# A sequence-model block with mixture-of-experts layers: from all eight experts for every token to the two chosen ones, sorted by expert through DRAM

## The chip, the cores and the metric

The kernel runs on one core of one Trainium2 chip. The metric is the device time of one execution in microseconds (us); a profiled execution is shown beside it, with the time from its first to its last instruction (the span).

The engines are named as in the profile: PE is the matmul engine, PEld its weight load, DVE the vector engine, ACT the engine of activations, POOL the engine that also builds descriptors for its own DMAs, SP the one that only issues DMAs and waits.

## The reference, cut to what matters

Sixteen sequences of 256 tokens, 128 features wide, go through an FFN, a mixer and a second FFN, with residual sums. Each FFN is a mixture of eight experts of which each token uses two; it is this part that the change rewrites.

```python
def ffn(x, gate_w, w1s, w2s):                 # x normalised; E = 8, D = 128, H = 512
    logits = xf @ gate_w
    probs = softmax(logits)
    vals, idx = top_k(probs, 2)
    vals = vals / sum(vals)                   # weights of the two chosen experts
    combine = zeros((N, E)).at[arange(N)[:, None], idx].add(vals)
    out = zeros_like(xf)
    for e in range(E):
        h = silu(xf @ w1s[e])
        out += combine[:, e:e + 1] * (h @ w2s[e])
    return out
```

The mixer is two Mamba blocks (a projection, a short convolution, a scan over time with 16 states for each of 256 channels, a projection back), the second with a small memory read on top:

```python
def step(h, ins):                             # over the 256 tokens of a sequence
    h = h * exp(d_t[:, :, None] * A) + (d_t * u_t)[:, :, None] * B_t[:, None, :]
    return h, einsum('bds,bs->bd', h, C_t)
```

## The kernel before, in words

Tokens are worked in eight groups of two sequences (512 tokens, four tiles of 128). A group has four slots, one for each sequence in each of the two Mamba blocks. The engines run programs written out by hand: `ORDER` gives for each engine, and each of the four slots, the order of its steps, and `run` plays the four slots for each group. Between engines there are only semaphores, and each engine keeps its order, so a step that waits holds all that stand behind it on its engine.

The scan of a slot is cut in eight steps j, each with two states for two halves of the channels (1024 elements in each of 128 partitions). For each j, ACT makes the decays (step `d`, line 621), PE spreads two rows over the partitions (steps `t`, line 403, into a ring of three banks `b_r`), and DVE does three large operations: the input product (`b`, line 900), the scan itself (`s`, line 910) and the output product (`g`, line 922). The output products of j = 1 to 7 are added by DMA: POOL issues one accumulating DMA for each (steps `a`, `pair_sum`, line 1098, 512 KB from `G` onto `acc`). Each of these waits until the one before it has landed, and `G` has three buffers (`NG = 3`), so the g step of j waits for the landing of an earlier one. The step `gate` (line 930) takes the finished sum of the slot before, so it waits for the seventh DMA.

Around the scan stand the small steps: on DVE `low`, `delta`, `xsum`, `un`, `lx`, `ln`, `unx`, `mask`, `xb`; on POOL the reciprocal roots `froot`, `rms`, `lnx`, `rmsx` (an add, a drain of the engine, and a power, lines 1066 and 1068) and the residual `rs`.

Sixteen FFNs (two for each group) are laid into the slots: the first stands alone ahead of the mixer (`start`), the last alone behind it (`finish`), and the fourteen others each take two slots. Of one FFN, before:

- DVE normalises (`fstats`, `fnorm`), takes the low part of the split tokens (`flow`), reads the logits (`flog`), takes the two largest (`ftop`) and makes an 8-wide row of weights (`fweights`).
- PE works in 64 pieces (steps `p`): for each expert four up pieces, each of three matmuls of 512 columns (the tokens and weights are split in a high and a low part), and four down pieces of 16 matmuls of 128 columns.
- ACT applies silu to 32 tiles of 512 columns (line 564).
- DVE adds each expert's result with the token's weight (`ffn_sum`, line 836): four operations for each of eight experts, from PSUM.

The weights of all experts stay in SBUF. PE, ACT and DVE run groups 1 to 5 as a loop (`Fori`); SP and POOL have them written out.

Of the kernel before, what the change touches and what calls it, by code (L numbers as in the profile page):

```python
# [5 lines left out]
P = 128  # L6
# [3 lines left out]
SEQ = 2  # L10
# [14 lines left out]
        ("outside", PAD)]  # L25
# [9 lines left out]
PAIR = 4 * HC  # L35
PIECES = E // 2 * PAIR

# [17 lines left out]
    ),  # L55
    "scalar": (
# [4 lines left out]
    ),  # L61
    "vector": (
# [35 lines left out]
def moe_mamba_kernel(nc, x, pack, early, sel, w1, w2, out):  # L98
# [4 lines left out]
    with ctx:  # L103
# [5 lines left out]
        raw = sb("raw", [P, E * HID])  # L109
        w1h = sb("w1h", [P, E, HID], fp32r)  # L110
        w1l = sb("w1l", [P, E, HID], fp32r)
        w2s = sb("w2s", [P, E, HC, D])
        selr = sb("selr", [P, 2 * DS, P], fp32r)
        ghl = sb("ghl", [P, 2, E], fp32r)
# [10 lines left out]
        def par(name):  # L125
# [13 lines left out]
        xh = sb("xh", [P, TOK], fp32r)  # L139
        xl = sb("xl", [P, TOK], fp32r)  # L140
# [65 lines left out]
        s_pack, s_w1, s_w2, s_sel, s_early, s_gate = (  # L206
            sem("s_pack"), sem("s_w1"), sem("s_w2"), sem("s_sel"), sem("s_early"), sem("s_gate"))
        s_raw_read, s_lg, s_Aexp, s_set_dve, s_set_act, s_exponent = (
            sem("s_raw_read"), sem("s_lg"), sem("s_Aexp"), sem("s_set_dve"), sem("s_set_act"),
            sem("s_exponent"))  # L210
        s_xin, s_store = sem("s_xin"), sem("s_store")

        f_stats, f_rstd, f_xn, f_xnT, f_split, f_logits, f_lread, f_gap, f_th, f_xh = (
            sem("f_stats"), sem("f_rstd"), sem("f_xn"), sem("f_xnT"), sem("f_split"),
            sem("f_logits"), sem("f_lread"), sem("f_gap"), sem("f_th"), sem("f_xh"))
        f_hmm, f_hact, f_ymm, f_yacc = sem("f_hmm"), sem("f_hact"), sem("f_ymm"), sem("f_yacc")
# [15 lines left out]

        def piece(k):

            pair, i = divmod(k, PAIR)
            down, i = divmod(i, 2 * HC)
            return bool(down), 2 * pair + i // HC, i % HC
# [25 lines left out]
        def _(sp):  # L263
# [16 lines left out]

            for g in range(GROUPS):
                if g + 1 < GROUPS:
                    sp.wait_ge(f_yacc, first(g) * E + 1)
                    sp.dma_start(xin[:, :, :], xt[g + 1]).then_inc(s_xin, 16)
                if g >= 2:
                    store(g - 2)
            store(GROUPS - 2)
            store(GROUPS - 1)
            sp.wait_ge(s_store, 16 * GROUPS)


        @block.tensor
        def _(pe):
# [34 lines left out]
            def ffn_down(n, e, j):  # L328
# [6 lines left out]
                if j == TILES - 1:  # L335
                    last.then_inc(f_ymm, 1)
# [869 lines left out]
```

## Time and profile before

| | us |
|---|---|
| median of three runs (1804.24 to 1805.67) | 1805.59 |
| the profiled execution's own time | 1800.28 |
| its span, first to last instruction | 1798.5 |
| DVE busy | 1585.3 (88%) |
| PE busy | 1472.0 (82%) |
| ACT busy | 1170.0 (65%) |
| POOL busy | 307.3 (17%) |

The profile has a page with shares, forty slices of the span and the costliest groups of instructions; behind it the trace can be asked for the instructions of a stretch, for who waited for whom, and for the DMAs. "Busy" counts instructions that compute; issuing a DMA counts on POOL alone. An engine that is idle and is not the bound costs nothing, so the shares tell where to look, and the waits tell what sets the end.

### The profile page before, as it was taken

To read this page: it belongs to the slowest core of one execution; us is meant where nothing else is said; L and a number is where in the kernel's file an instruction comes from. 1 tells how busy PE (TensorE), PEld (TensorE's weight loads), DVE (VectorE), ACT (ScalarE), POOL (GpSimd) and SP (SyncE) were. 2 spreads that over 40 slices of the span, in tenths; PEclk is the share of its full clock that TensorE was granted. 3 is DMA by queue.
4 is the path that set the end of the run, shared out by engine and by line. 5 is a ranking of instruction groups with operands and counts; after the bars stand their busy time and mean duration, and the time that the engine had idled before them with its cause. 6 is when DMAs were issued, how large, how long until landed. Compare 5 with 4: busy or idle time off the path is not lost. (4 is left out here: it accounts for less than half of the span.)

```text
span 1798.5 us, 26359 instructions
## 1 busy us (share of the span) xinstructions
PE 1472.0 (82%) x8672; PEld 1260.7 (70%) x8672; DVE 1585.3 (88%) x2421; ACT 1170.0 (65%) x2227; POOL 307.3 (17%) x366
## 2 busy tenths in 40 slices
PE   5878666888989888988889788888889898568768
PEld 4767545777777778777778678776778677447657
DVE  5249999999999999999999999999999999999821
ACT  3267555866866777866876677856876677558422
POOL 0001121122112221122112121122112121111100
PEclk9988866998999899998999899998999899569979
DMA  5004444433443334433443334433344334443400
GB/s 198 1 12 82 77 82 82 88 71 59 83 84 71 71 71 90 89 71 60 80 87 67 74 72 90 87 68 62 74 80 78 67 75 89 82 82 73 94 5 7
DMA packets 43947, 131.93 MB, mean 73 GB/s; under 512 B 3984, under 2 KB 12176, under 8 KB 43664
## 3 DMA queue, kind: packets, MB, share of 16 engines
q0 software_dynamic: 32256, 117.45, 34.4%
q1 hardware_dynamic: 11536, 12.56, 2.2%
q8 instruction: 79, 1.29, 0.3%
q14 instruction: 76, 0.62, 0.1%
HBM read 10.46 MB, written 2.10 MB: 7 GB/s over the span
## 5 line engine op out<-in xcount | busy, mean ns | idle before, releaser
L910 DVE TENSOR_TENSOR_SCAN hs<-dA,dbu 128x1024 f32<-128x1024 f32 x256 | 584.3, 2288 | 5.2 <-issue 3.6
L564 ACT ACTIVATE raw<-b_h 128x512 f32<-128x512 f32 x512 | 304.2, 599 | 268.4 <-PE b_h L326 255.7
L621 ACT ACTIVATE dA<-delta,A 128x255 f32<-128x255 f32 x1024 | 421.7, 495 | 12.1 <-DVE hs L910 9.9
L1098 POOL DMA_DIRECT2D acc<-G x224 | 195.9, 875 | 1028.8 <-DVE G L922 583.5
L403 PE MATMUL b_r<-bcr,selr 128*128 128x256 f32 x1024 | 243.9, 334 | 124.7 <-DVE G L922 65.8
L324 PE MATMUL b_h<-xh,w1h 128*128 128x512 f32 x512 | 247.9, 484 | 82.1 <-DVE ob L836 29.3
L900 DVE TENSOR_TENSOR dbu<-du,b_r 128x1024 f32<-128x1024 f32 x256 | 306.2, 1206 | 6.6 <-PE b_r L403 4.3
L403 PEld LDWEIGHTS b_r<-bcr,selr 128*128 128x128 f32 x1024 | 177.3, 207 | 166.9 <-DVE G L922 75.3
L922 DVE TENSOR_TENSOR G<-hs,b_r 128x1024 f32<-128x1024 f32 x224 | 272.0, 1214 | 7.1 <-issue 5.0
L333 PE MATMUL b_out<-w2s,raw 128*128 128x128 f32 x2048 | 252.2, 275 | 0.0
L333 PE MATMUL b_h<-w2s,raw 128*128 128x128 f32 x2048 | 250.2, 275 | 0.0
L333 PEld LDWEIGHTS b_out<-w2s,raw 128*128 128x128 f32 x2048 | 244.8, 192 | 4.1
L333 PEld LDWEIGHTS b_h<-w2s,raw 128*128 128x128 f32 x2048 | 241.1, 192 | 1.1
L326 PE MATMUL b_h<-xh,w1l 128*128 128x512 f32 x512 | 219.8, 429 | 0.0
L325 PE MATMUL b_h<-xl,w1h 128*128 128x512 f32 x512 | 219.6, 429 | 0.0
L324 PEld LDWEIGHTS b_h<-xh,w1h 128*128 128x128 f32 x512 | 107.0, 209 | 159.8 <-ACT raw L564 71.5
L361 PE MATMUL b_w<-uT,inx 128*128 128x256 f32 x512 | 153.4, 440 | 9.4 <-ACT ez L610 4.5
L326 PEld LDWEIGHTS b_h<-xh,w1l 128*128 128x128 f32 x512 | 107.1, 209 | 26.7
L361 PEld LDWEIGHTS b_w<-uT,inx 128*128 128x128 f32 x512 | 103.9, 220 | 24.5 <-ACT uT L574 6.1
L325 PEld LDWEIGHTS b_h<-xl,w1h 128*128 128x128 f32 x512 | 109.0, 213 | 9.0
L621 ACT ACT_TABLE_LOAD x86 | 110.3, 1283 | 1.5
L564 ACT ACT_TABLE_LOAD x44 | 56.5, 1283 | 24.3 <-PE b_h L326 23.7
(144 smaller groups left out, 1551.6 us busy)
## 6 DMA issues: line engine op xcount, KB each, us to landing
acc<-G POOLq DMA_DIRECT2D x224, 512.0 KB, 4.5
xin<-x_dram SPq DMA_DIRECT2D x8, 256.0 KB, 2.8
raw<-w_dram SPq DMA_DIRECT2D x1, 2048.0 KB, 10.9
out_dram<-ob SPq DMA_DIRECT2D x8, 256.0 KB, 2.9
prm<-pack_dram SPq DMA_DIRECT2D x1, 1124.5 KB, 5.2
hs<-sel_dram SPq DMA_DIRECT2D x2, 512.0 KB, 12.3
G<-sel_dram SPq DMA_DIRECT2D x2, 512.0 KB, 7.5
dA<-early_dram SPq DMA_DIRECT2D x1, 512.0 KB, 11.4
```

The costliest lines, as they stand in the source:

```text
L324: mm(h, w1h[:, e, w], xh[:, :], start=True, stop=False)
L325: mm(h, w1h[:, e, w], xl[:, :], start=False, stop=False)
L326: mm(h, w1l[:, e, w], xh[:, :], start=False, stop=True).then_inc(f_hmm, 1)
L333: last = mm(EOUT[e % 2][:, j * D:(j + 1) * D], hT[e % 2][:, c, j * P:(j + 1) * P], w2s[:, e, c, :], start=c == 0, stop=c == HC - 1)
L361: last = mm(o, inx[:, m, r, ch], uT[:, b, PAD - r:PAD - r + T], start=r == 0, stop=r == PAD)
L403: last = mm(R[ring(i, t)][:, d * T:(d + 1) * T], selr[:, kind * DS + DP * j + d, :], bcr[b][:, :], start=True, stop=True)
L564: do(hT[e % 2][:, c, :], H[i % 2][:, :], ACT.Silu).then_inc(f_hact, 1)
L621: last = do(dA[j % 4][:, d, k, 1:], delta[b][:, k, 1:], ACT.Exp, scale=A[:, k, s:s + 1])
L900: V.tensor_tensor(dbu[j % 2][:, :, :, :], du[i % 2][:, :, :].unsqueeze(1).broadcast_to([P, DP, HALVES, T]), spread_rows(i, (0, j)), ALU.mu ...
L910: V.tensor_tensor_scan(flat(hs[j % 2]), flat(dA[j % 4]), flat(dbu[j % 2]), 0.0, ALU.mult, ALU.add)\
L922: V.tensor_tensor(to[:, :, :, :], hs[j % 2][:, :, :, :], spread_rows(i, (1, j)), ALU.mult)\
L1098: Q.dma_start(acc[b][:, :, :, :].rearrange("p d h t -> p (d h t)"), G[j % NG][:, :, :, :].rearrange("p d h t -> p (d h t)"), accum_op=ALU. ...
```

## The change

Each FFN computes each token for its two experts only. Its parts:

- The first matmul runs in full fp32, no longer in split parts; the copies `w1h`, `w1l`, `xh`, `xl` and the operations that make them go.
- After the two largest logits, DVE makes a 0/1 mask, PE counts by matmul how many tokens come before each one at each expert, and DVE works out a place for each (token, expert) pair in a list of `NT` = 15 tiles of 128 rows in which each expert starts on a tile of its own (`ffn_place`), and the expert of each tile (`eid`).
- POOL scatters the 4 x 128 normalised tokens to their two places in DRAM with eight indirect DMAs (`ffn_scatter`, 64 KB each), after which SP loads the sorted list back in five chunks of three tiles (`chunk_in`).
- For each of the 15 tiles SP reads the expert's number from SBUF into a register and loads that expert's first weight, 256 KB, from DRAM into a ring of four (`expert_in`); PE turns the tiles (15 transposes), does 4 up matmuls of 128 columns, reads the expert's number into a register, and does 4 down matmuls; ACT does 15 silus and 10 copies from PSUM.
- SP writes the results to DRAM in five chunks (`chunk_out`), and POOL gathers them back with eight indirect DMAs (`ffn_gather`). DVE adds them with 8 operations from SBUF in place of 32 from PSUM.
- Routing (norm, logits, places, scatter) now stands in the slot before the two that hold the matmul pieces, and the sums stand at the end of the second of these. All four `ORDER` lists are new. POOL has 7 accumulating DMAs in every slot as before, and 16 indirect ones more in slots 1 and 3.
- POOL copies the residual once for each FFN (`ffn_keep`), and the two sorted lists are cleared once at the start. The loop on PE, ACT and DVE is written out.

```diff
-        "rms a1 rs froot a2 a3 a4 a5 a6 a7",
-        "rms a1 rs lnx a2 a3 rmsx a4 a5 a6 a7",
-        "a1 a2 froot a3 a4 a5 a6 a7",
+        "froot a1 a2 sc0 sc1 sc2 sc3 sc4 sc5 fkeep rms a3 sc6 sc7 a4 ga0 ga1 ga2 ga3 ga4 a5 ga5 ga6 ga7 rs a6 a7",
+        "rms a1 a2 a3 rs a4 lnx a5 rmsx a6 a7",
+        "froot sc0 sc1 sc2 a1 a2 sc3 sc4 a3 sc5 a4 sc6 ga0 ga1 ga2 sc7 ga3 a5 ga4 ga5 ga6 ga7 a6 fkeep a7",
...
+        "b0 b1 s0 s1 g0 gate b2 g1 s2 b3 b4 s3 g2 low s4 g3 delta b5 mask g4 s5 b6 g5 b7 xb s6 s7 g6 g7",
+        "b0 b1 s0 fstats s1 g0 b2 fnorm s2 flog g1 ftop b3 fplace g2 gate s3 xsum b4 b5 g3 un s4 g4 b6 s5 s6 g5 "
+        "b7 g6 fweights s7 low g7 fsum delta",
+        "b0 b1 s0 b2 g0 gate s1 xsum g1 b3 un s2 lx g2 s3 b4 g3 s4 b5 g4 s5 b6 g5 s6 ln low g6 b7 unx delta s7 g7",
+        "fstats b0 b1 fnorm s0 flog b2 ftop g0 fplace s1 g1 s2 b3 g2 gate s3 b4 g3 s4 b5 g4 s5 low b6 g5 b7 s6 "
+        "delta mask g6 s7 fweights g7 fsum xb",
...
             def ffn_up(n, e, c):
...
-                mm(h, w1h[:, e, w], xh[:, :], start=True, stop=False)
-                mm(h, w1h[:, e, w], xl[:, :], start=False, stop=False)
-                mm(h, w1l[:, e, w], xh[:, :], start=False, stop=True).then_inc(f_hmm, 1)
+            def ffn_up(n, i):
+                r, k, t = RING_OF["U", i], n * NT + i, i % CH * P
+                pe.wait_ge(s_w[k % NW], 16 * (k // NW + 1))
+                wait(pe, f_hact, n * ITEMS + max(r - 1, RING_OF["T", i // CH] + 1))
                 for c in range(HC):
+                    w = slice(c * P, (c + 1) * P)
+                    last = mm(H[r % 2][:, w], wst[k % NW][:, w], xsT[i // CH % 2][:, t:t + P], start=True, stop=True)
+                last.then_inc(f_hmm, 1)
+
+            def ffn_down(n, i):
+                pe.wait_ge(f_hact, n * ITEMS + RING_OF["U", i] + 1)
...
+                e = pe.value_load(eid[n % 2][0:1, i:i + 1], min_val=0, max_val=E - 1)
+                for c in range(HC):
+                    last = mm(Y[:, i % CH * D:(i % CH + 1) * D], hT[i % NH][:, c, :], w2s[:, e, c, :],
+                              start=c == 0, stop=c == HC - 1)
+                last.then_inc(f_ymm, 1)
...
+            def ffn_sum(f):
+
+                n, src, dst, g, is_first = f
+                dve.wait_ge(s_gat, 16 * 2 * TILES * (n + 1))
...
                 for k in range(2):
...
+                    for j in range(TILES):
+                        last = V.scalar_tensor_tensor(
+                            out=dst[:, j, :], in0=yk[:, k, j, :], scalar=c01[n % 2][:, k, j:j + 1], in1=dst[:, j, :],
+                            op0=ALU.mult, op1=ALU.add)
...
+            def ffn_scatter(n, x):
+                k, j = divmod(x, TILES)
+                if x == 0:
+                    pool.wait_ge(f_pos, n + 1)
+                    pool.wait_ge(s_zero, 32)
+                Q.indirect_dma_start(xs_d[n % 2], bass.IndirectOffsetOnAxis(ap=posi[n % 2][:, x:x + 1], axis=0),
+                                     xn[:, j, :], None).then_inc(s_scat, 16)
+
+            def ffn_gather(n, x):
+                k, j = divmod(x, TILES)
+                if x == 0:
+                    wait(pool, f_yacc, n)
+                    for c in range(CHUNKS):
+                        pool.wait_ge(s_ys[c], 16 * (n + 1))
+                Q.indirect_dma_start(yk[:, k, j, :], None, ys_d[n % 2],
+                                     bass.IndirectOffsetOnAxis(ap=posi[n % 2][:, x:x + 1], axis=0)).then_inc(s_gat, 16)
```

## Rows read from the trace of the kernel before

**Rows 1.** Windows of the span: busy us of each engine, clock, DMA share, GB/s.
```profile
0.00:114.00 114.00, 74.32 (x414) 60.47 (x415) 37.82 (x136) 35.63 (x60) 6.34 (x17) 0.92 0.23 79
114.00:1705.00 1591.00, 1328.52 (x7861) 1143.92 (x7861) 1529.45 (x2212) 1112.07 (x2130) 298.87 (x346) 0.90 0.40 77
```

**Rows 2.** Timeline of SP, stores of successive groups: start, us, engine, line, operation.
```profile
505.89 0.39 SPq L279 DMA_DIRECT2D out_dram<-ob  x1
...
1114.85 0.38 SPq L279 DMA_DIRECT2D out_dram<-ob  x1
```

**Rows 3.** DVE: groups by line of the middle stretch, then its timeline in one slot.
```profile
L910 DVE TENSOR_TENSOR_SCAN hs<-dA,dbu 128x1024 f32<-128x1024 f32 x256 | 584.3, 2288 | 5.2 <-issue 3.6 <-ACT dA L621 0.2
L922 DVE TENSOR_TENSOR G<-hs,b_r 128x1024 f32<-128x1024 f32 x224 | 272.0, 1214 | 7.1 <-issue 5.0 <-DVE hs L910 1.0 <-DMA acc<-G 0.4
...
914.84 0.68 DVE L788 TENSOR_TENSOR xl<-b_out,xh 128x512 fp32r<-128x512 f32 x1
...
928.67 0.19 DVE L824 TENSOR_TENSOR comb<-hit 128x32 f32<-128x32 f32 x1
...
937.50 1.12 DVE L836 SCALAR_TENSOR_TENSOR xa<-b_out,comb,xin 128x128 f32<-128x128 f32 x4
938.54 1.21 DVE L922 TENSOR_TENSOR G<-hs,b_r 128x1024 f32<-128x1024 f32 x1
```

**Rows 4.** A slot that holds no FFN: its window, POOL's timeline, and DVE's gate behind it.
```profile
268.50:308.40 39.90, 24.00 (x93) 19.55 (x94) 37.85 (x37) 22.80 (x50) 7.59 (x9) 0.66 0.49 93
...
277.34 0.86 POOL L1098 DMA_DIRECT2D acc<-G  x1 [4.18 <-DMA acc<-G]
...
282.23 1.04 POOL L1068 TENSOR_TENSOR rstd<-rstd,powh 128x4 f32<-128x4 f32 x1 [3.58 <-DMA acc<-G]
283.23 0.89 POOL L1098 DMA_DIRECT2D acc<-G  x1
288.36 0.86 POOL L1098 DMA_DIRECT2D acc<-G  x1 [4.24 <-DMA acc<-G]
...
308.36 0.69 DVE L930 TENSOR_TENSOR yg<-acc 128x512 f32<-128x512 f32 x1 [0.64 <-DMA acc<-G]
```

**Rows 5.** DMA queue and issues; last row: accumulates beside a store, 904 to 916 us.
```profile
q0 software_dynamic: 32256, 117.45, 34.4%
...
acc<-G POOLq DMA_DIRECT2D x224, 512.0 KB, 4.5
xin<-x_dram SPq DMA_DIRECT2D x8, 256.0 KB, 2.8
...
DMA to landing us min/median/max: 4.9/5.2/5.4
```

**Rows 6.** POOL's adds at line 1066, two of one shape: ns min/median/max.
```profile
L1066 POOL TENSOR_TENSOR rstdm<-mvm,epst x7: 2238/2242/2247, 226.8 to 1437.2; 128x4 f32<-128x4 f32 x7
L1066 POOL TENSOR_TENSOR rstdr<-vr,epst x7: 201/201/203, 244.1 to 1456.6; 128x4 f32<-128x4 f32 x7
```

**Rows 7.** ACT by line: silu and the table loads ahead of it.
```profile
L564 ACT ACTIVATE raw<-b_h 128x512 f32<-128x512 f32 x512 | 304.2, 599 | 268.4 <-PE b_h L326 255.7
...
L564 ACT ACT_TABLE_LOAD x44 | 56.5, 1283 | 24.3 <-PE b_h L326 23.7
```

**Rows 8.** The FFN alone at the start, DVE: normalised, last sum, first scan input.
```profile
9.61 1.12 DVE L780 TENSOR_SCALAR xn<-xin,mv,rstd 128x128 f32<-128x128 f32 x4 [1.19 <-POOL rstd L1068]
...
84.32 1.13 DVE L836 SCALAR_TENSOR_TENSOR xa<-b_h,comb,xa 128x128 f32<-128x128 f32 x4 [2.45 <-PE b_h L333]
...
114.16 1.22 DVE L900 TENSOR_TENSOR dbu<-du,b_r 128x1024 f32<-128x1024 f32 x1
```

**Rows 9.** The FFN alone at the end: DVE normalised and last sum, PE 32 down matmuls.
```profile
1728.76 1.12 DVE L780 TENSOR_SCALAR xn<-xb,mv,rstd 128x128 f32<-128x128 f32 x4 [2.64 <-POOL rstd L1068]
...
1793.78 1.13 DVE L836 SCALAR_TENSOR_TENSOR ob<-b_h,comb,ob 128x128 f32<-128x128 f32 x4 [2.45 <-PE b_h L333]
...
1743.41 3.73 PE L333 MATMUL b_out<-w2s,raw 128*128 128x128 f32 x32
```

More of the change, by code:

```diff
@@ L24 @@
         ("out_b_row", D), ("ident", P), ("dist", T), ("causal", T), ("iota", E), ("tap_b", DI), ("ones_row", P),
-        ("outside", PAD)]
+        ("outside", PAD), ("before", P), ("steps", TILES), ("tiles", 15), ("ones_e", E)]
 DP = 2
@@ L277, in store, with chunk_out, load_x @@
+            def chunk_out(n, c):
+                wait(sp, s_gat, 16 * 2 * TILES * (n - 1))
+                sp.wait_ge(f_ys, n * CHUNKS + c + 1)
+                sp.dma_start(rows(ys_d[n % 2], c), ys[:, c * CH:(c + 1) * CH, :]).then_inc(s_ys[c], 16)
+            def load_x(g):
+                sp.wait_ge(f_keep, first(g - 1) + 1)
+                sp.wait_ge(f_xn, first(g - 1) + 1)
+                sp.dma_start(xin[:, :, :], xt[g]).then_inc(s_xin, 16)
             def store(g):
-                sp.wait_ge(f_yacc, (second(g) + 1) * E)
+                sp.wait_ge(f_yacc, second(g) + 1)
@@ L279, in store @@
                 sp.dma_start(ot[g], ob[:, :, :]).then_inc(s_store, 16)
[L281 to L287, printed above, removed]
+            firsts = {first(g): g for g in range(GROUPS)}
+            seconds = {second(g): g for g in range(GROUPS)}
+            for n in range(2 * GROUPS):
+                for i in range(NW):
+                    expert_in(n, i)
+                if n in seconds and n - 1 in seconds:
+                    store(seconds[n - 1])
+                for c in range(CHUNKS):
+                    chunk_in(n, c)
+                if n in firsts and firsts[n] + 1 < GROUPS:
+                    load_x(firsts[n] + 1)
+                if n in firsts and n - 1 in seconds:
+                    store(seconds[n - 1])
+                for i in range(NW, NT):
+                    expert_in(n, i)
+                    if i >= CH + 5 and i % CH == 2:
+                        chunk_out(n, (i - 5) // CH - 1)
+                for c in range((NT - 1 - 5) // CH, CHUNKS):
+                    chunk_out(n, c)
@@ L342, in turn @@
                 wait(pe, q_sp, 4 * g + i)
+                if i == 0 and 0 < g < GROUPS - 1:
+                    pe.wait_ge(f_tile, first(g + 1) + 1)
+                elif i == 2 and g > 0:
+                    pe.wait_ge(f_tile, second(g - 1) + 1)
                 for j in tiles:
@@ L525, in _ @@
             run(0, first(1), None, first(2), False)
-            with pe.Fori(1, GROUPS - 2) as g:
+            for g in range(1, GROUPS - 2):
                 run(g, g * 2, g * 2 + 1, g * 2 + 2, False)
@@ L691, in _ @@
             run(0, first(1), None, first(2), False)
-            with act.Fori(1, GROUPS - 2) as g:
+            for g in range(1, GROUPS - 2):
                 run(g, g * 2, g * 2 + 1, g * 2 + 2, False)
@@ L1049, in _ @@
             run(0, first(1), None, first(2), False)
-            with dve.Fori(1, GROUPS - 2) as g:
+            for g in range(1, GROUPS - 2):
                 run(g, g * 2, g * 2 + 1, g * 2 + 2, False)
@@ L1107, in residual, with slot @@
                 Q.tensor_tensor(rs[:, tiles, :], xam[:, tiles, :], x1[:, tiles, :], ALU.add).then_inc(g_rs, 1)
-            def slot(g, i, tail, head, n, nx, nxt):
+            def slot(g, i, tail, head, f, fx, nxt):
                 for name, num in steps("gpsimd", i):
@@ L1139, in run @@
                     head = (g, i + 1) if i < 3 else None if is_last else (g + 1, 0)
-                    slot(g, i, tail, head, (n1, n2)[i // 2], (n2, n3)[i // 2], None if is_last else g + 1)
+                    slot(g, i, tail, head, (f1, f2)[i // 2], (f2, f3)[i // 2], None if is_last else g + 1)
             start()
@@ L1177 @@
         "gate": a("ffn_gate_w"),
+        "before": (np.arange(P)[None, :] > s).astype(f), "ones_e": np.ones((P, E), f),
+        "steps": np.broadcast_to(P * np.arange(TILES, dtype=f), (P, TILES)),
+        "tiles": np.broadcast_to(np.arange(NT, dtype=f), (P, NT)),
         "xp": rows(np.concatenate([bc, xp[:DR].T], 1)), "out_w": rows(a("attn_out_proj_w").T),
```

444 lines of the change are left out of this document (272 added, 172 removed), and 26 rows, old and new, of the table ORDER.

## The prediction

> **What bounds the kernel now.** I read the windows of the span first. The kernel has a head until the first scan input at 114 us, a middle to 1705 us, and a tail. In the middle DVE is busy 1529 of 1591 us, PE 1329, ACT 1112, POOL 299 [rows 1]: DVE is the bound there, at 96%. The reader is to see that PE, which loses most work by the change, is not. Then SP's timeline, for the period: three groups pass between the stores at 505.89 and 1114.85 us, so a group takes 203.0 us, a slot 50.7 [rows 2]. Then DVE by line and in order: the scan is 2.29 us, the two products 1.21 each, and neighbours overlap by some 0.09 us (four sums take 1.12 us and the next operation starts 1.04 after them) [rows 3]. So one j is about 4.45 us, eight are 35.6: 70% of a slot is scan that no part of the change touches.
>
> The third view matters most: the one slot of the middle where PE has no FFN and DVE hardly any. It runs at a granted clock of 0.66 with PE busy 24 of 39.9 us, and DVE is still busy 37.9; but the accumulating DMAs go back to back, 5.13 us from 283.23 to 288.36, and the gate behind them waits 0.64 us for the last [rows 4]. So just below DVE lies a second bound: the chain of seven DMAs, each of which waits for the landing of the last. At 5.05 us each it needs 35 us, and with what stands between the gate and a1 a slot can't be shorter than about 39. One more thing is seen there: POOL's power at 282.23 waited 3.58 us for the DMA issued ahead of it, and that pair of issues is 5.89 apart. A root on POOL (add, drain, power) finishes only when DMAs issued before it have landed.
>
> **DVE's own work, per FFN.** Removed: 32 sums, 8 x 1.04 = 8.3 us, of which 8 come back as sums from SBUF, taken at the same 0.26 each = 2.1. Removed: the low part, 0.6 with overlap; one read of logits and the two products with the weights, about 0.75 (four small operations of 0.19 with drains) [rows 3]. Added: some ten small operations in the place step with a drain between most, at 0.19 plus 0.08 each, about 2.4. Net 8.3 + 0.6 + 0.75 - 2.1 - 2.4 = 5.2 us saved, 10.4 for a group. PE loses most of its FFN: 57 us of matmuls become about 15, since 32 matmuls of the down kind take 3.73 us and there are now 120 of them and 15 transposes [rows 9]. As DVE is the bound, that alone gives nothing.
>
> From this, and the new order, DVE's slots without any wait are: slot 0, 40.5 us; slot 1, 50.4; slot 2, 44.8; slot 3, 49.2. Sum 185. The FFN's DVE work stands in slots 1 and 3 alone, so 0 and 2 come close to the floor of 39.
>
> **What the chain of DMAs becomes.** Three new loads fall on it.
>
> (a) Traffic. For each FFN there are 15 weight loads of 256 KB, 1.97 MB of chunks in and out, and 1.05 MB scattered and gathered: 6.9 MB, 27 transfers of 256 KB, 13.3 for a slot. A store of 256 KB beside the accumulates raised their landing from 4.5 us to 5.4 at most [rows 5]: up to 0.9 us for one. An accumulate holds the DMA engines for 2.76 us (34.4% of 1798.5 over 224) [rows 5], seven are 19.3 of 50 us, so 39% of 13.3 x 0.9 = 12 us meets them: 4.6 us for a slot, 0.65 for each. Bounds: 0 (all transfers fall in gaps) and 1.15 (in proportion to the time in flight). I take 0.65: landing 5.15, period 5.7.
>
> (b) Sixteen indirect issues in slots 1 and 3. The nearest row is the direct issue on POOL, 0.86 us [rows 4]. An indirect one must also fetch 128 numbers, so it isn't cheaper. The upper bound is from POOL's adds: the same 128x4 add takes 201 ns in one place and 2242 in another, where DVE runs a scan [rows 6]. If a fetch were held so, on half of the issues, one would be 1.9. I take 1.1, near the direct row. The Trainium skill (SBUF — State Buffer, Who interferes with whom) says that a DVE instruction with two SBUF inputs contends with a GpSimd one that reads SBUF, and that the second to issue blocks; the two rows agree. By that rule, if it holds for index fetches, 1.9 is the price and the time is that of the second rival. Landing of an indirect DMA: none is shown; the nearest is 2.8 us for 256 KB [rows 5], which I take.
>
> (c) The roots. They now stand behind the last accumulate of the slot before, or behind scatters.
>
> Now the four slots, times from each slot's start. Slot 0: gate ends about 9.9, g1 at 12; a7 is issued at 12 + 6 x 5.7 = 46.2, which is 5.7 in slot 1, and lands at 10.9. froot ends a microsecond later, 11.9; DVE wants fnorm at 10.0: wait 1.9. Slot 1: about one microsecond each of round trip to PE before flog and before fplace; places at 23.7, a2 at 24.8, six scatters to 32.3, their landing 35.1, the root of `rms` to 36.1 (un waits 1.5), a3 there, a4 at 41.8, five gathers to 48.2, a5, three gathers to 52.4, landed 55.2. DVE wants fsum at 52.2: wait 3.0. Slot 1 = 50.4 + 2 + 1.9 + 1.5 + 3.0 = 58.8. Slot 2: g1 at 14.2; lnx and rmsx add 2.5 to the chain; a7 at 50.9, 6.1 into slot 3, lands 11.3; froot 12.3. DVE wants fnorm at 3.4, since fstats opens the slot: wait 8.9. This is the largest new wait; behind it on DVE stand the whole scan of slot 3 and, on PE, the turn, the logits and the counts. Slot 3: places at 24.1, three scatters to 27.4, a1 27.4, a2 33.1, a3 38.8, a4 44.5, six indirect ones to 52, a5, four gathers to 57.3, landed 60.1; DVE wants fsum at 57.5: wait 2.6. Slot 3 = 49.2 + 2 + 8.9 + 2.6 = 62.7. Sum 40.5 + 58.8 + 44.8 + 62.7 = 206.8 against 203.0: +3.8 for a group. What is idle as dispatch gaps today (some 5 us of a group) I count as covered by the new waits. The middle has 32 slots less those with less FFN, about seven such groups: **+27 us**.
>
> **Head and tail.** At the tail, from xn to the last sum, now 1729.9 to 1794.9 = 65.0 us [rows 9]. After: turn, gate, top, counts, places about 11; eight scatters 8.8 and landing 2.8; chunk in 3.2; 15 tiles; chunk out 3.2; eight gathers 8.8 and landing 2.8; sum 2.1. A tile: up 0.45 (4 x 0.117, less overlap), silu 0.6 and two semaphore hops 0.3 [rows 7], the register load, down 0.45. No row shows a register load on PE; bounds 0 and 1.5 (then SP, with one load and one issue of 0.4 for each tile, would bind as well), taken 0.9: 2.7 for a tile, 40.5, with turns and copies 42.5. Sum 85.4: **+20**. The Trainium skill (DMA: Bandwidth & Descriptors, Latency and other measured facts) has about 600 ns as the floor of a tensor load; with 0.6 the two lone FFNs are 9 us cheaper in all. At the head the same 85.4 from xn at 10.7 ends at 96.1, before 85.5 [rows 8]: +10.6; the second FFN's routing now lies between the norm and the first turn of the mixer, 5.5 less the 2.3 of norm work moved ahead: **+14** in all. Clearing the lists (2 x 0.98 MB) stands ahead of the other loads on SP's queue but lands before the places are known.
>
> Work that is hidden: the ten copies and the silus on ACT (15 x 0.6 + 10 x 0.4 in place of 32 x 0.6); table loads rise by my count from 25 to 36 for a group, 11 x 1.28 = 14 us more on an engine that is busy 70% [rows 7, 1]. In slot 1 ACT would then be busy 45 of 59 us: covered, and without that cover up to 7 us for a slot. The lower clock: covered, as the slot at 0.66 shows [rows 4].
>
> **Sum.** 27 + 20 + 14 = 61. On the profiled execution's 1800.3 that is 1861; the median stands 5 above it, so 1866 us, +3.4%.
>
> **Rivals.**
> - *The chain keeps its pace (faster).* Issue 0.86, no traffic met: the same walk gives waits of 2 and 0.6 in slot 1, 4.3 and 2 in slot 3, slots 40.5 + 53 + 44.8 + 55.5 = 193.8, seven times -9.2 = -64, head and tail +24: 1766. For it: DMA engines are busy 40% only [rows 1]. Against: the chain had no slack in the slot without FFN [rows 4], and slots 0 and 2 become such slots. It decides at about 0.3 us of traffic for each accumulate with 1.0 for an issue; there the group is near 199 and the time 1806, no change.
> - *Indirect issues are held (much slower).* At 1.9 each, 0.8 more on 16 issues puts about 11 us into each of slots 1 and 3: +150 in the middle, +26 at the ends: 2040. At 1.5, 1950.
> - *PE's register loads hold the spread rows.* 15 loads of 1.5 us with the waits ahead of them put 11 us into each slot of PE, in order with the `t` steps. PE has 20 us to spare in a slot, but where five pieces stand ahead of t0 a bank can be late by 3 us: +80 over the middle, 1945 if all else is as forecast.
> - *It doesn't do what it says:* if the PE work did not fall, nothing of the middle would change beyond the above, as DVE binds; this would show in PE's busy time only.
>
> **How the numbers follow.** Forecast (chain late by some, 1820 to 1930) 0.50; chain keeps its pace 0.32 (with 0.27 below 1802); held issues 0.10; PE 0.08. A run can tell 0.2%, 3.6 us. Within it falls little from either side: 0.05. Faster 0.30, slower 0.65. The range reaches from the first rival, 1755 with cheap register loads, to 1960 (held issues at 1.5); beyond it remain the issues above 1.5 us and some of the first rival's best.
>
> **What would show it.** Right: DVE's wait at fnorm, on POOL's root, and at the sum, on gathers, are the largest of the middle; accumulates land in over 5 us; DVE busy about 70 us less in the middle; PE busy under 900. Wrong: indirect issues under 0.9 or over 1.5 on POOL; DVE waiting for `b_r`; head and tail moved by less than 15 or more than 60 together.

## The result and the profile after

The changed kernel takes 2034.28 us (median of 2033.62 to 2043.89); the kernel before, on the same chip, 1805.63. The ratio is 1.127, with an interval from 1.124 to 1.131: slower, by 229 us where +61 was forecast, and outside the range. The profiled execution has a span of 2032.8 us.

| us | before | after |
|---|---|---|
| DVE busy | 1585.3 (88%) | 1497.6 (74%) |
| PE busy | 1472.0 (82%) | 1292.5 (64%) |
| ACT busy | 1170.0 (65%) | 1176.6 (58%) |
| POOL busy | 307.3 (17%) | 640.0 (31%) |
| start to the first scan input | 114.2 | 130.5 |
| from there to the last norm (`xn`) | 1614.6 | 1810.4 |
| from there to the end of the last sum | 66.2 | 89.2 |

The three last rows (each from where the one above ends) say where the 234 us between the two spans lie: 16 at the head, 196 in the middle, 23 at the tail. Head and tail were forecast at 14 and 20; the middle at 27. The windows of after answer to [rows 1], columns as there:

```profile
0.00:130.50 130.50, 57.93 (x356) 52.41 (x356) 29.62 (x147) 31.17 (x55) 33.94 (x44) 0.84 0.47 143
130.50:1912.00 1781.50, 1185.79 (x6705) 1052.07 (x6704) 1453.40 (x1933) 1128.58 (x2106) 586.37 (x574) 0.79 0.55 121
1912.00:2032.80 120.80, 48.78 (x317) 44.51 (x317) 14.55 (x66) 16.88 (x31) 19.65 (x22) 0.67 0.27 72
```

DVE's busy time in the middle fell by 76 us (third number with its count: 1453.40 against 1529.45; 73 between the same two steps, first scan input and last norm, 1460.51 against 1533.87). It is now busy 82% of the middle, and no other engine is busier: none is the bound by its work alone. So the next view is that of the waits. First the length of a group, from DVE's gates two groups apart (timeline):

```profile
638.05 0.68 DVE L1040 TENSOR_TENSOR yg<-acc 128x512 f32<-128x512 f32 x1
...
1104.20 0.68 DVE L1040 TENSOR_TENSOR yg<-acc 128x512 f32<-128x512 f32 x1
```

That is 233.1 us a group against 203.0 in [rows 2] and 206.8 forecast. The window of just these two groups:

```profile
638.05:1104.20 466.15, 317.49 (x1847) 283.86 (x1846) 371.37 (x530) 297.86 (x551) 164.65 (x158) 0.81 0.56 126
```

What DVE waited for in it (line, releaser: us in total, times, longest):

```profile
DVE ob L945 <- DMA yk<-results,posi: 21.9, 2, 11.3
DVE xn L874 <- POOL rstd L1173: 12.9, 4, 3.9
DVE xa L945 <- DMA yk<-results,posi: 12.2, 2, 6.3
DVE un L976 <- POOL rstdr L1173: 8.4, 4, 4.9
DVE lg L880 <- PE b_w L386: 6.3, 4, 1.6
DVE un L976 <- issue: 6.2, 2, 3.2
DVE more L905 <- PE b_w L397: 5.8, 4, 2.1
DVE ln L959 <- POOL rstdm L1173: 4.4, 2, 2.7
DVE acc L1032 <- PE b_r L500: 3.7, 2, 2.2
```

DVE is busy 371.37 / 2 = 185.7 us of a group (the forecast's slots without waits sum to 185). The waits are 86.2 / 2 = 43.1, forecast 21.9; 4.3 more lie between its instructions. The largest are the sums on the gathered rows (`ob`, `xa`: 17.0 us a group). The norms on POOL's roots follow: `un`, 7.3, and `xn`, 6.5. (The `un` waits marked `issue` belong there: they are 22.3 us in the whole trace, and 3.4 in `e4_own_sem` below, whose roots have no drain.) `b_r` is small. POOL stands behind sums and norms. Its groups by line (busy us, mean ns, idle before with releasers), and then its timeline in a slot 3:

```profile
L1230 POOL DMA_DIRECT2D acc<-G x224 | 204.1, 911 | 822.8 <-DMA acc<-G 427.0 <-DVE G L1032 395.4 <-issue 0.3
L1194 POOL DMA_INDIRECT sorted<-xn,posi x128 | 178.7, 1396 | 140.4 <-DVE posi L928 104.0 <-issue 36.4
L1203 POOL DMA_INDIRECT yk<-results,posi x128 | 162.1, 1267 | 117.8 <-DMA results<-ys 80.0 <-issue 36.0 <-DMA acc<-G 1.8
```

```profile
731.17 0.20 POOL L1171 TENSOR_TENSOR rstd<-mv,epst 128x4 f32<-128x4 f32 x1
734.87 1.03 POOL L1173 TENSOR_TENSOR rstd<-rstd,powh 128x4 f32<-128x4 f32 x1 [3.50 <-issue]
748.93 2.87 POOL L1194 DMA_INDIRECT sorted<-xn,posi  x1 [13.03 <-DVE posi L928]
752.11 1.01 POOL L1194 DMA_INDIRECT sorted<-xn,posi  x1 [0.30 <-issue]
...
762.10 1.05 POOL L1194 DMA_INDIRECT sorted<-xn,posi  x1 [0.30 <-issue]
763.45 3.04 POOL L1194 DMA_INDIRECT sorted<-xn,posi  x1 [0.30 <-issue]
766.49 0.99 POOL L1230 DMA_DIRECT2D acc<-G  x1
...
790.15 0.95 POOL L1203 DMA_INDIRECT yk<-results,posi  x1 [0.30 <-issue]
```

And DVE in the same stretch:

```profile
748.60 2.29 DVE L1020 TENSOR_TENSOR_SCAN hs<-dA,dbu 128x1024 f32<-128x1024 f32 x1
...
763.37 2.28 DVE L1020 TENSOR_TENSOR_SCAN hs<-dA,dbu 128x1024 f32<-128x1024 f32 x1
...
794.15 2.35 DVE L945 SCALAR_TENSOR_TENSOR ob<-yk,c,ob 128x128 f32<-128x128 f32 x8 [11.28 <-DMA yk<-results,posi]
```

Two things are to be seen. The scatter at 763.45 starts just after the scan at 763.37 and takes 3.04 us, to 0.84 us past the scan's end; its neighbour at 762.10, with no scan, takes 1.05. Over the whole trace, 61 of the 256 indirect issues start in a scan and have a mean of 2.41 us; the 195 others have 0.99, and only one of these is over 1.2 (1.99, at 27.77, beside `scalar_tensor_tensor` operations of DVE). To each comes a gap of 0.30 us. So an issue costs 1.33 + 0.30 = 1.63 us on average, and the last gather of this slot is issued at 790.15, when DVE has been waiting for it since 782.87. The second thing: the root's power at 734.87 idles 3.50 us behind an add that ended at 731.37. The last sign of landing of the accumulate issued just ahead of it, at 730.16, comes 0.2 us before the power starts. In the kernel before, 14 such powers start 0.17 or 0.38 us after the landing of the accumulate issued ahead of them.

### The profile page after: what moved, and what is told of

Read it like the earlier page. It is cut to its first block and busy times, and to the rows that moved or that the text cites. A ratio compares the mean times of both kernels' runs of the same rounds, so it can differ in the third digit from the quotient of the medians.

```text
span 2032.8 us, 26140 instructions
## 1 busy us (share of the span) xinstructions
PE 1292.5 (64%) x7376; PEld 1149.0 (57%) x7376; DVE 1497.6 (74%) x2145; ACT 1176.6 (58%) x2191; POOL 640.0 (31%) x639
## 5 line engine op out<-in xcount | busy, mean ns | idle before, releaser
L423 PE MATMUL b_out<-w2s,hT 128*128 x1920 | 296.4, 303 | 72.0 <-issue 45.9
L414 PE MATMUL b_h<-xsT,wst 128*128 128x128 f32 x1920 | 303.6, 310 | 57.6 <-ACT xsT L667 40.8
L414 PEld LDWEIGHTS b_h<-xsT,wst 128*128 128x128 f32 x1920 | 280.2, 224 | 65.9 <-issue 65.6
L423 PEld LDWEIGHTS b_out<-w2s,hT 128*128 128x128 f32 x1920 | 266.8, 215 | 88.2 <-issue 87.8
L1010 DVE TENSOR_TENSOR dbu<-du,b_r 128x1024 f32<-128x1024 f32 x256 | 305.8, 1209 | 14.6 <-PE b_r L500 10.7
L670 ACT ACTIVATE hT<-b_h 128x512 f32<-128x512 f32 x240 | 140.7, 598 | 172.9 <-PE b_h L414 164.6
L458 PE MATMUL b_w<-uT,inx 128*128 128x256 f32 x512 | 178.9, 497 | 69.8 <-DVE xb L1070 61.7
L1194 POOL DMA_INDIRECT sorted<-xn,posi x128 | 178.7, 1396 | 140.4 <-DVE posi L928 104.0
L1203 POOL DMA_INDIRECT yk<-results,posi x128 | 162.1, 1267 | 117.8 <-DMA results<-ys 80.0
L667 ACT ACTIVATE xsT<-b_h 128x384 f32<-128x384 f32 x80 | 38.7, 484 | 156.8 <-PE b_h L405 156.6
L945 DVE SCALAR_TENSOR_TENSOR ob<-yk,c,ob 128x128 f32<-128x128 f32 x64 | 19.0, 358 | 134.7 <-DMA yk<-results,posi 134.1
L405 PE MATMUL b_h<-prm,xsort 128*128 128x128 f32 x240 | 49.4, 324 | 65.1 <-DMA xsort<-sorted 43.1
```

Source lines behind the costliest of these rows:

```text
L414: last = mm(H[r % 2][:, w], wst[k % NW][:, w], xsT[i // CH % 2][:, t:t + P], start=True, stop=True)
L423: last = mm(Y[:, i % CH * D:(i % CH + 1) * D], hT[i % NH][:, c, :], w2s[:, e, c, :], start=c == 0, stop=c == HC - 1)
L458: last = mm(o, inx[:, m, r, ch], uT[:, b, PAD - r:PAD - r + T], start=r == 0, stop=r == PAD)
L670: do(hT[k % NH][:, :, :], H[r % 2][:, :].rearrange("p (c t) -> p c t", c=HC), ACT.Silu)\
L1010: V.tensor_tensor(dbu[j % 2][:, :, :, :], du[i % 2][:, :, :].unsqueeze(1).broadcast_to([P, DP, HALVES, T]), spread_rows(i, (0, j)), ALU.mu ...
L1194: Q.indirect_dma_start(xs_d[n % 2], bass.IndirectOffsetOnAxis(ap=posi[n % 2][:, x:x + 1], axis=0), xn[:, j, :], None).then_inc(s_scat, 16)
```

## Experiments

Theory 1: the price of the indirect issues on POOL, held by scans, is what was underrated. Theory 2: it is the added traffic. Theory 3: the drains in POOL's roots wait for landings (the drain stands between the add and the power that reads its result). A fourth is that PE or SP is late.

**Plain DMAs in place of the indirect ones** (from the changed kernel):

```diff
-                Q.indirect_dma_start(xs_d[n % 2], bass.IndirectOffsetOnAxis(ap=posi[n % 2][:, x:x + 1], axis=0),
-                                     xn[:, j, :], None).then_inc(s_scat, 16)
+                Q.dma_start(xs_d[n % 2][x * P:(x + 1) * P, :], xn[:, j, :]).then_inc(s_scat, 16)
```

> Edit: the 16 indirect DMAs of each FFN become plain DMAs of the same size from the same POOL steps, to and from fixed rows. Left out: the sorting itself (each pair goes to row x*128 of the list), so the output is not the reference's; routing, counts, loads and matmuls stay. Theory 1 (held issues: an indirect issue costs 1.27 to 1.40 us plus a 0.30 gap, because its index fetch is held by DVE's scans): plain issues cost 0.9, so 16 x 0.7 = 11 us leave each of slots 1 and 3, 22 for a group of 233, 2034 becomes about 1880; no issue over 1.1 us. Theory 2 (traffic: the added transfers lengthen landings): no change, 2030 +-10. Theory 3 (the drains in POOL's roots wait for landings): no change, 2030 +-10.

1910.44 us, ratio to before 1.060 (1.055 to 1.064): 124 us came back, of 154 expected. An issue now takes 0.76 us (scatter) and 0.74 (gather) on average, at most 0.91, and has no gap; the 122 that start in a scan take 0.77, the others 0.73. Of the waits for the sums in the middle, those of `ob` are all but gone (65.0 us in all, of which 62.3 are the lone tail; in the changed kernel 134.1 and 73.4), those of `xa` fell from 43.5 to 28.1. Theory 1 holds; theories 2 and 3 alone fall.

**The same plain DMAs on SP** (8 ahead of the weight loads, 8 behind the last chunk out):

```diff
+                sp.wait_ge(f_pos, n + 1)
...
+                for y in range(2 * TILES):
+                    sp.dma_start(xs_d[n % 2][y * P:(y + 1) * P, :], xn[:, y % TILES, :]).then_inc(s_scat, 16)
                 for i in range(NW):
                     expert_in(n, i)
...
```

> Edit: the same plain DMAs, issued by SP instead of POOL: 8 of scatter size ahead of the weight loads of an FFN, 8 of gather size behind its last chunk. Left out: the sorting, as in e1_direct. Traffic is the same, POOL has none of the issues. Theory 1: 16 x 1.65 = 26 us leave POOL's queue in slots 1 and 3; the group falls to about 200 and the time to 1780 to 1810. Theory 2: no change, 2030 +-15. Theory 3: the roots still wait for accumulates, so at most 10 us of a group, about 1960.

1946.04 us (1.079): 88 us came back, but the time is 136 to 166 us over what was expected, and worse than leaving them on POOL. The expectation looked at the queue that is relieved, not at the one that is loaded. SP now stands waiting for the places (`f_pos`) and for landed results, and the chunks and weights for PE stand behind. PE's waits:

```profile
PE b_h L416 <- DMA xsort<-sorted: 109.4, 10, 15.3
```

and DVE's, for a spread row of PE:

```profile
DVE dbu L1021 <- PE b_r L511: 69.8, 21, 12.3
```

In the changed kernel PE waits 43.1 us for `xsort` and DVE 10.7 for this `b_r`. It says nothing against theory 1, and shows that the fourth rival can be made true by a misplaced wait.

**Less traffic** (weight loads after the first four move a quarter, which takes away 2.9 of the 6.9 MB that an FFN adds):

```diff
-                sp.dma_start(wst[k % NW][:, :], w1[e]).then_inc(s_w[k % NW], 16)
...
+                    sp.dma_start(wst[k % NW][0:32, :], w1[e][0:32, :]).then_inc(s_w[k % NW], 16)
```

> Edit: all weight loads after the first four move 32 of 128 partitions (64 KB in place of 256). Left out: three quarters of each expert's up weights stay those of an earlier tile, so the output is not the reference's. 15 x 0.19 = 2.9 MB of the 6.9 MB that an FFN adds are gone. Theory 2: accumulates land sooner and the waits on POOL and for chunks shrink by 40%: 1940 or less. Theories 1 and 3: 2015 to 2035.

2007.61 us (1.112): 27 us. This part of the traffic is a small cost. The other 4 MB stayed; if they cost the same per MB, all of it is some 64 us (27 x 6.9 / 2.9, an estimate that no run tests). From POOL's timelines, the time from one accumulate to the next where the second waited for the first: mean 5.26 us before, 5.68 after, 5.48 here. The forecast took 5.7.

**The roots without drains** (`s` is a semaphore that only this root uses, `k` its count so far):

```diff
-                Q.tensor_tensor(r[:, tiles], v, epst[:, tiles], ALU.add)
-                pool.drain()
+                Q.tensor_tensor(r[:, tiles], v, epst[:, tiles], ALU.add).then_inc(s, 1)
+                pool.wait_ge(s, k)
                 return Q.tensor_tensor(r[:, tiles], r[:, tiles], powh[:, tiles], ALU.pow)
```

> Edit: in each root on POOL the drain between the add and the power (and the two in the entry root) becomes an increment on the add and a wait for it, with semaphores of their own; arithmetic unchanged. Theory 3 (a drain also waits until the DMA issued before has landed, 3.5 to 4.9 us in the trace): the roots end 4 us sooner; of the waits of DVE on roots (fnorm, un, ln: some 16 us of a group) most go: 2034 becomes about 1930. Theory 1: DVE waits for the gathers instead; at most 5 us of a group come back, 2000. Theory 2: no change.

1943.42 us (1.078, 1.074 to 1.082): 91 us, near the 104 that theory 3 expected. The idle time before the power of `rstd` went from 60.1 us to 1.3, and DVE's wait at the norm `xn` from 53.9 to 9.1. POOL's group in the changed kernel:

```profile
L1173 POOL TENSOR_TENSOR rstd<-rstd,powh 128x4 f32<-128x4 f32 x16 | 16.7, 1043 | 60.1 <-issue 60.0
```

The same group in this kernel:

```profile
L1174 POOL TENSOR_TENSOR rstd<-rstd,powh 128x4 f32<-128x4 f32 x16 | 16.7, 1042 | 1.3
```

And DVE's wait for it here:

```profile
DVE xn L875 <- POOL rstd L1174: 9.1, 8, 1.7
```

So both theories hold. Are they one cost or two?

**Both edits together** (`e1_direct` and `e4_own_sem`):

```diff
-                pool.drain()
+                pool.wait_ge(s, k)
...
-                Q.indirect_dma_start(yk[:, k, j, :], None, ys_d[n % 2],
-                                     bass.IndirectOffsetOnAxis(ap=posi[n % 2][:, x:x + 1], axis=0)).then_inc(s_gat, 16)
+                Q.dma_start(yk[:, k, j, :], ys_d[n % 2][x * P:(x + 1) * P, :]).then_inc(s_gat, 16)
```

> Edit: e1_direct and e4_own_sem together (plain DMAs in place of the indirect ones, the drains of the roots replaced). Left out: the sorting, as in e1_direct. If issues and roots are two separate costs, the gains add: 2034 - 124 - 91 = 1819. If both remove the same wait, one of them hides the other: 1900. If nothing else of the change costs anything in the middle, what is left over the kernel before is head and tail, +30, less up to 70 us of DVE work that went: 1770 to 1836.

1827.55 us (1.012): 207 us came back, 124 + 91 = 215 if they simply add. They are two costs. In its trace the middle, from the first scan input (117.83) to the last norm (1736.74), is 1618.9 us; before it was 1614.6 and in the changed kernel 1810.4. With each edit alone it is 1707.4 and 1710.4. The two take the middle back to 4 us over before; the head is then 4 us and the tail 13 longer than before. But DVE has 77 us less to do in this middle than before (1456.62 against 1533.87), and none of that shows in the time. It is used up by other waits, of which the largest are the sums (30.9 us in the middle) and the two round trips to PE (36.2). No run separates these from the traffic.

**The sums later,** from the end of slots 1 and 3 to behind the next gate, on `e4_own_sem`:

```diff
-        "b7 g6 fweights s7 low g7 fsum delta",
...
+        "b7 g6 fweights s7 low g7 delta",
...
-        "b0 b1 s0 b2 g0 gate s1 xsum g1 b3 un s2 lx g2 s3 b4 g3 s4 b5 g4 s5 b6 g5 s6 ln low g6 b7 unx delta s7 g7",
+        "b0 b1 s0 b2 g0 gate fsum s1 xsum g1 b3 un s2 lx g2 s3 b4 g3 s4 b5 g4 s5 b6 g5 s6 ln low g6 b7 unx delta s7 g7",
```

> Edit: on e4_own_sem, DVE's weighted sums on the gathered rows go from the end of slot 1 and 3 to behind the gate of the next slot. All arithmetic stays. If the wait of the sums on the gathers (12 and 22 us in two groups, 17 of a group, the largest of the trace) is what is left of the middle's excess, most of it goes: 1943 - 7 x 14 = 1845 (1830 to 1880). If the chain of accumulates behind the late issues on POOL sets the slot anyway, the wait moves to the gate: 1930 to 1943.

1952.14 us (1.079) against 1943.42: nothing gained. The wait moved to the gate, where the last accumulates are late behind the gathers; it was 8.7 us in `e4_own_sem`:

```profile
DVE yg L1041 <- DMA acc<-G: 97.8, 15, 12.7
```

The largest wait of DVE was a symptom of how late POOL's queue runs: to move the sum alone moves the wait.

**Issues added to the kernel before.** 16 in each slot 1 and 3, 256 in all, nobody waits for them; first indirect, then plain:

```diff
-        "rms a1 rs froot a2 a3 a4 a5 a6 a7",
+        "rms a1 rs froot a2 x0 x1 x2 x3 x4 x5 a3 x6 x7 a4 x8 x9 x10 x11 x12 a5 x13 x14 x15 a6 a7",
...
+                Q.indirect_dma_start(scratch, at, w2s[:, x % 8, x // 8, :], None).then_inc(s_extra, 16)
```

and in `e11_before_plain`, in place of the last line:

```diff
+                Q.dma_start(scratch[x * P:(x + 1) * P, :], w2s[:, x % 8, x // 8, :]).then_inc(s_extra, 16)
```

> Edit: on the kernel before, 16 indirect DMAs that nobody waits for (128 rows of 512 B each from a constant tile to a scratch list) in each of slots 1 and 3, placed between the accumulates as the changed kernel has them. Nothing is left out, only added. Theory 1 (DVE's scans hold the index fetch): a mean of 1.25 to 1.45 us for one, the longest 3.0 (a fetch and a whole scan); six in one 4.2 us gap of the chain and five in another push the chain by 10 us in slots that have 12 to spare: +10 to +60. Rival (the long issues of the changed kernel come from full DMA queues or its extra traffic, not from DVE): mean under 1.1, none over 2; +0 to +15.

> Edit: e8_before_issues with plain DMAs of the same rows in place of the 256 indirect ones, nothing else. If the price in e8 (148 us for 256) is POOL's time in the issue (1.38 + 0.30 each), a plain one at 0.75 without the gap costs under half: 256 x 0.93 = 238 us of POOL's queue are gone, and the time falls to 1810 to 1850. If it is the transfers themselves, on the queue that the accumulates use: 1940 to 1955 again.

The indirect ones cost +148 us (1953.03; 1.080, 1.077 to 1.084), the plain ones +37 (1843.49; ratio 1.022, with 1806.13 for before in that set). The mean issue is 1.38 us with the 0.30 gap, against 0.84 without one (1.25 to 1.45 and 0.75 expected). The time of the plain ones was as expected; that of the indirect ones was expected too low by 88 us or more. I had reckoned with 12 us of slack in such a slot. POOL's group in `e8_before_issues`:

```profile
L1072 POOL DMA_INDIRECT scratch<-w2s,index x256 | 352.4, 1377 | 77.3 <-issue 75.4 <-DMA acc<-G 1.8
```

And where the price is paid, DVE's gate waiting for the last accumulate (12.9 us with the plain issues, 8.9 in the kernel before):

```profile
DVE yg L933 <- DMA acc<-G: 133.1, 17, 13.2
```

Here the accumulates a2 to a5 of one slot start at 841.28, 852.76, 858.52 and 866.93 us, so three steps of the chain take 25.7 us where 15 would do. The chain can win back little of that: it needs 5.0 us for a step, and in a slot that is not disturbed DVE gives it a product every 5.5 to 6.5 (784.86 to 808.89), so most of a delay is carried to the gate. This is read from the trace; no run isolated it.

**No scan beside the fetches** (from the changed kernel):

```diff
-                V.tensor_tensor_scan(flat(hs[j % 2]), flat(dA[j % 4]), flat(dbu[j % 2]), 0.0, ALU.mult, ALU.add)\
+                V.tensor_reduce(flat(hs[j % 2])[:, 0:1], flat(dA[j % 4]), mybir.AxisListType.X, ALU.add)
+                V.tensor_reduce(flat(hs[j % 2])[:, 1:2], flat(dbu[j % 2]), mybir.AxisListType.X, ALU.add)\
```

> Edit: on the changed kernel each scan (two inputs from SBUF, 2.29 us) becomes two reductions of 1024 elements with one SBUF input each. Left out: the recurrence itself (the products then use a cleared tile), so the output is not the reference's. Theory 1 (it is the scan that holds the index fetch): the indirect issues fall from a mean of 1.33 to 1.0 us, and almost none is over 1.2 (60 of 256 are now); the few left stand beside sums of two SBUF tiles. Rival (any long DVE instruction, or the DMA queue, makes them long): 50 or more over 1.2, mean 1.3. The time itself tells little, as the reductions may be shorter than the scan.

In its trace the mean issue is 1.00 us, the longest 1.99, six of 256 are over 1.2 (60 in the changed kernel), and all six start beside another DVE operation on two tiles in SBUF (`inx`, `delta`, `yg`):

```profile
L1197 POOL DMA_INDIRECT sorted<-xn,posi x128 | 130.1, 1016 | 142.7 <-DVE posi L930 106.3 <-issue 36.1 <-DMA acc<-G 0.3
L1206 POOL DMA_INDIRECT yk<-results,posi x128 | 126.6, 989 | 117.2 <-DMA results<-ys 79.6 <-issue 37.7
...
L1022 DVE TENSOR_REDUCE hs<-dA 128x1 f32<-128x1024 f32 x256 | 310.4, 1212 | 3.3 <-ACT dA L728 1.5 <-issue 1.4
```

DVE is as busy there, even a little longer (two reductions of 1.21 us against a scan of 2.28), and reads the same two tiles; it is the scan, not a busy DVE, that holds the issue. The time is 1973.11 us (two executions), 61 less, though DVE has 256 x 0.14 = 36 us more to do. The 0.30 us gaps stay. The Trainium skill (SBUF — State Buffer, Who interferes with whom) says that a DVE instruction with two SBUF inputs contends with a GpSimd instruction that reads SBUF, and that a `tensor_reduce` never does on trn2. This pair of runs agrees (1.33 us beside scans, 1.00 beside reductions), if the fetch of an indirect DMA's indices is such a read.

**Spreading the gathers.** On `e4_own_sem`, those of slot 3 go to slot 0 of the next group, two behind an accumulate, with their sums behind the fifth product; SP's store of the output goes behind the ninth weight load (POOL's order, against the changed kernel):

```diff
-        "a1 a2 a3 a4 a5 a6 a7",
+        "a1 ga0 ga1 a2 ga2 ga3 a3 ga4 ga5 a4 ga6 ga7 a5 a6 a7",
...
-        "froot sc0 sc1 sc2 a1 a2 sc3 sc4 a3 sc5 a4 sc6 ga0 ga1 ga2 sc7 ga3 a5 ga4 ga5 ga6 ga7 a6 fkeep a7",
+        "froot sc0 sc1 sc2 a1 sc3 sc4 a2 sc5 sc6 a3 sc7 a4 a5 a6 fkeep a7",
```

> Edit: on e4_own_sem, the eight gathers of slot 3 go to slot 0 of the next group, two behind each accumulate, and their weighted sums to the middle of that slot; slot 3 keeps its eight scatters, at most two behind one accumulate; SP's store goes behind the ninth weight load. All arithmetic stays. If clumps of issues between two accumulates are the price (three to eight in one gap of 4.2 us, where two and a half fit), slot 3 loses the 11 us wait of its sums and slot 0 gains none: 1943 - 7 x 10 = 1870 (1850 to 1890). If the chain has no slack wherever the issues stand, each still delays it and the gate waits: 1930 to 1955.

1950.47 us (1.080), no gain, as the second case has it, but not for its reason: the gate waits only 29.1 us in all. In slot 0 DVE asks for the sums before the gathers can be there (POOL's last gather, then DVE's sum):

```profile
1012.53 0.98 POOL L1209 DMA_INDIRECT yk<-results,posi  x1 [0.30 <-issue]
...
1017.70 2.35 DVE L946 SCALAR_TENSOR_TENSOR ob<-yk,c,ob 128x128 f32<-128x128 f32 x8 [10.48 <-DMA yk<-results,posi]
```

**The same, sums two products later** (DVE's order in slot 0, against the changed kernel):

```diff
-        "b0 b1 s0 s1 g0 gate b2 g1 s2 b3 b4 s3 g2 low s4 g3 delta b5 mask g4 fsum s5 b6 g5 b7 xb s6 s7 g6 g7",
+        "b0 b1 s0 s1 g0 gate b2 g1 s2 b3 b4 s3 g2 low s4 g3 delta b5 mask g4 s5 b6 g5 b7 xb s6 s7 g6 fsum g7",
```

> Edit: e10_spread with the weighted sums of slot 0 moved from behind the fifth to behind the seventh product. In e10_spread DVE wants the sums at 1007.2 us, the last gather is issued at 1012.53 and has landed at 1017.70: the sums were asked for 10.5 us too early in each of six groups, and that wait hid what spreading gives. If so, this one is at 1950 - 6 x 9 = 1896 (1880 to 1915). If the chain of accumulates has no slack in slot 0 (gate waits 4.4 us in e10_spread already), the wait goes to the gate of slot 1: 1940 to 1955.

1908.01 us (1.059, 1.057 to 1.060): 35 us better than `e4_own_sem`. The wait for `ob` fell from 134.1 us in 7 to 74.9 in 2, one of them the lone tail. So spreading the gathers pays only with the sum moved as far as they were. That clumps of issues between two accumulates are what cost the 35 us fits this, but the store's move came with it and no run separates the two.

**The drains, in the kernel before:** the edit of `e4_own_sem` in the old file.

```diff
-                pool.drain()
+                pool.wait_ge(s, k)
```

> Edit: on the kernel before, the drains in POOL's roots become increments and waits of their own; arithmetic unchanged. The trace of before has 41 us in which rstd's power waits for a landing, but DVE waits only 8 us for it: 0 to -8, 1800. If the roots were a price of the kernel before too, -30.

1795.36 us, ratio 0.994 (0.992 to 0.996): a little faster than the kernel before, and the fastest of all kernels here; the arithmetic is unchanged. DVE's wait at `xn` falls from 8.0 us to 3.0. The drains were nearly free before, since DVE hardly waited for them; in the changed kernel it waits 53.9 us at `xn` alone.

## Why the prediction was wrong

*What bounds the kernel, and where the change costs.* Right: DVE's work falls by about 70 us in the middle (73 to 76), nothing comes of it, since waits on the chain of accumulates and POOL's queue take its place, and the sums are the largest wait of the middle (99.2 us). The norm `xn`, named with them, is at 47.4, no more than `un` (47.7). Of the signs of being wrong, `b_r` is there with 3.2 us a group; the issue itself, 1.33 us, stays under the 1.5 that was to show it, because the sign left out the gap.

*Head and tail.* 34 forecast, 39 measured, and that is partly luck, as the parts at the tail show. Routing to the first scatter took 20.7 us for 11, because the residual's copy ahead of the scatters waits for a store, which SP issues behind the first weight loads. The tiles were cheaper, 43.7 us from the last scatter to the first gather where the terms gave 51.7 (2.8 + 3.2 + 42.5 + 3.2): a tile took 2.2 us (14 in 31.1, from 1978.2 to 2009.3) for 2.7, though its matmuls were dearer than taken (see below). Eight scatters took 10.0 us for 8.8; gathers and sum 13.7, as forecast. The misses largely cancel.

*(a) Traffic.* The period was right, 5.7 us forecast and 5.68 measured. The term wasn't quite: by the same mean the kernel before has 5.26 where the forecast started from 5.05, so the chain got 0.42 us slower for each accumulate, not 0.65.

*(b) Indirect issues: the step that failed.* "I take 1.1, near the direct row." It is 1.63: 0.99 for an issue left alone, 0.30 of gap that no row of before showed, and 0.34 from the scans. Plain issues in their place give back 124 of the 229 us. The evidence stood in [rows 6], an add of 201 ns that takes 2242 beside a scan, and the prediction made of it a rival with a chance of 0.10; it names the mechanism, its effect and, by its walk, 2040 us. But it set that at 1.9 each; at 1.63 its own two points give some 1980. That its total is near the measured 2034 is luck: the price was too high and other waits were too low. The choice of 1.1 had only a row of another operation for it, an issue that has no indices to fetch. The rule that the prediction cited from the Trainium skill (SBUF — State Buffer, Who interferes with whom) spoke for the other row, and `e9_no_scan` bears it out: without the scans the mean issue falls from 1.33 to 1.00 us.

*(c) The roots.* Root waits were forecast at 12.3 us a group, `fnorm` 10.8 and `un` 1.5; measured are 6.5, 7.3 and 2.2 at `ln`, 16.0. The mechanism, a root that ends only behind a landing, was right and the sum a quarter too small; the places were not. The wait at `fnorm` in slot 3, "the largest new wait" at 8.9 us, is 2.6 in both groups shown, that in slot 1 is 3.7 and 3.9 for 1.9. The wait for roots was counted as a fact of the kernel; `e4_own_sem` shows that it was an effect of the drain, and 91 us could be had back.

*The walk through the slots.* Per group, forecast and measured: sums on gathers 5.6 and 17.0; roots 12.3 and 16.0; the two round trips to PE 4 and 6.1; `b_r` 0 and 3.2; gaps between instructions "covered", measured 4.3; the rest under 1. These make 21.9 and 47.4, so the group is 233.1 in place of 206.8. The landing of a gather was right: from the issue at 790.15 to the sum 4.0 us, forecast 1.1 + 2.8 = 3.9.

*Slack of the chain.* The walk had each delay of POOL swallowed by the 4.2 us in which it waits for a landing. `e8_before_issues` shows how little that is worth where issues come in clumps: 148 us for 256 issues. This is a second mis-sized term of the same step.

*PE.* "PE busy under 900" is wrong: 1292.5. Up and down matmuls and the turns make 303.6 + 296.4 + 49.4 us, 41 for an FFN, forecast 15. The 32 rows in 3.73 us of [rows 9] were counted as 32 matmuls. But the four matmuls that each tile has in either step show as eight rows in the trace of after (x1920 for 16 x 15 x 4), so the 32 rows were 16 matmuls, and a matmul is twice as dear. (In the kernel before, a down piece has four of them, 16 for an expert, not 16 for a piece.) The rest of the miss stays open. In the middle it changed little, as PE isn't the bound there.

```profile
L414 PE MATMUL b_h<-xsT,wst 128*128 128x128 f32 x1920 | 303.6, 310 | 57.6 <-ACT xsT L667 40.8 <-ACT hT L670 16.5
L423 PE MATMUL b_out<-w2s,hT 128*128 x1920 | 296.4, 303 | 72.0 <-issue 45.9 <-ACT hT L670 22.1 <-ACT ys L662 3.7
```

*The other rivals.* The chain didn't keep its pace (its 1766 stood on 0.86 us for an issue and no traffic met). Even with plain issues and no drains the kernel stands at 1827.55, 1.2% over before. PE held the spread rows only a little: DVE waits 3.2 us a group for `b_r`, where the rival had 11 us in each slot of PE; whether register loads cause it is not shown.

*The range.* Its upper end, 1960, was set by "held issues at 1.5". With the bound of 1.9 that the text itself derived, it had to reach 2040.

## What to carry to other kernels

Work taken off the bound engine is worth only what the next queue lets through: before moving rows through DRAM with indirect DMAs, count the issues on the queue that has to make them (here at 1.3 us each, plus what DVE's scans hold), and see what is queued behind them. If one row of the trace shows a thing being held tenfold by an overlap, price the new thing with the hold, until a reason speaks against it. On POOL, when it issues DMAs, try a semaphore of its own in place of a drain, and when a transfer is moved, move what consumes it as far.

## What was not expected of the hardware

- An indirect issue on POOL has a gap of 0.30 us ahead of it that a plain one hasn't, and isn't shorter than 0.94 us.
- Plain issues on POOL aren't held by scans: 128 scatters of `e1_direct` took 537 to 902 ns each, where the indirect ones of the changed kernel took 957 to 3040.
- POOL's drain between two of its own instructions waits until the DMAs issued ahead have landed (3.50 us at 734.87); a semaphore on the first instruction doesn't (1.3 us in all for 16 roots).
- The granted clock was 0.79 in the middle, 0.90 before, with PE busy 67% in place of 84%.
